# A decoder layer's cross attention with queries instead of keys held stationary, and its three programs joined into one

## The reference

```python
# 16 query heads, 4 key heads, HEAD_DIM 128; q and k normed and turned, k_full = context + own keys
scores = jnp.einsum('blhd,bmhd->bhlm', q, k_full) * scale + mask      # mask: 0 for context, causal for own keys
probs = jax.nn.softmax(scores, axis=-1)
out = jnp.einsum('bhlm,bmhd->blhd', probs, v_full)
```

## Time and profile before

| | us |
|---|---|
| median of 3 runs | 2986.56 |
| the profiled execution, its own time | 2984.8 |
| its span | 2982.8 |
| TensorE (PE) busy | 2906.3 (97%) |
| VectorE (DVE) busy | 1384.0 (46%) |
| ScalarE (ACT) busy | 1034.6 (35%) |
| GpSimd (POOL) busy | 186.6 (6%) |

### The profile page before, as it was taken

The page is one execution under the profiler, slowest core; times in us unless marked ns, Lnnn a source line. Parts: engine busy times, 40 slices in busy tenths (PEclk is TensorE's granted clock), DMA queues, the critical chain, the costliest instruction groups (busy, mean ns, idle before and its releaser), DMA issues. The chain is left out here.

```text
span 2982.8 us, 40563 instructions
## 1 busy us (share of the span) xinstructions
PE 2906.3 (97%) x15836; PEld 2775.5 (93%) x15836; DVE 1384.0 (46%) x1683; ACT 1034.6 (35%) x1499; POOL 186.6 (6%) x213
## 2 busy tenths in 40 slices
PE   8999999999999999999899999999999999999998
PEld 7899888899999999899799999999899999999997
DVE  3322233344454444578788888834522222222235
ACT  4322233332222223234476766722311121221222
POOL 0000000000000000200022322201000000000001
PEclk9999999999999999999899999999999999999999
DMA  4232223211111111022111112112111211111122
GB/s 170 87 108 81 79 79 129 74 49 56 43 47 52 56 44 69 29 88 69 53 62 57 56 61 63 40 53 102 57 56 56 71 56 57 60 67 56 56 72 99
DMA packets 88106, 203.03 MB, mean 68 GB/s; under 512 B 9376, under 2 KB 64260, under 8 KB 73832
## 3 DMA queue, kind: packets, MB, share of 16 engines
q1 hardware_dynamic: 88040, 202.12, 20.3%
HBM read 171.89 MB, written 30.21 MB: 68 GB/s over the span
## 5 line engine op out<-in xcount | busy, mean ns | idle before, releaser
L116 PE MATMUL PS<-XH,WH 128*128 128x400 f32 x2176 | 755.4, 347 | 10.6 <-DVE t_ROOM L1846 6.6
L118 PE MATMUL PS<-XH,WL 128*128 128x400 f32 x2176 | 746.5, 343 | 0.0
L117 PE MATMUL PS<-XL,WH 128*128 128x400 f32 x2048 | 703.5, 343 | 0.0
L116 PEld LDWEIGHTS PS<-XH,WH 128*128 128x128 f32 x2176 | 410.5, 189 | 15.8 <-issue 8.6
L118 PEld LDWEIGHTS PS<-XH,WL 128*128 128x128 f32 x2176 | 409.1, 188 | 0.1
L117 PEld LDWEIGHTS PS<-XL,WH 128*128 128x128 f32 x2048 | 384.5, 188 | 0.0
L1608 DVE TENSOR_TENSOR WL<-RAW,WH 128x1024 fp32r<-128x1024 f32 x86 | 105.4, 1225 | 524.2 <-ACT WH L1602 524.2
L86 ACT ACTIVATE WH<-RAW 128x1024 fp32r<-128x1024 f32 x120 | 126.9, 1058 | 552.0 <-PE PS L118 367.8
L92 DVE TENSOR_TENSOR WL<-RAW,WH 128x1024 fp32r<-128x1024 f32 x120 | 146.8, 1224 | 321.2 <-ACT WH L86 320.0
L1602 ACT ACTIVATE WH<-RAW 128x1024 fp32r<-128x1024 f32 x86 | 91.1, 1059 | 535.3 <-PE PS L118 530.4
L1560 DVE TENSOR_TENSOR XL<-a_E,XH 128x400 fp32r<-128x400 f32 (+1 forms) x224 | 174.0, 796 | 22.0 <-ACT XH L1504 22.0
(11 more groups left out here) (250 smaller groups left out, 5367.8 us busy)
## 6 DMA issues: line engine op xcount, KB each, us to landing
RAW<-weights_dram SPq DMA_DIRECT2D x111, 1024.0 KB, 4.8
a_KRAW<-keys_scratch SPq DMA_DIRECT2D x32, 411.0 KB, 3.3
a_VRAW<-values_scratch SPq DMA_DIRECT2D x32, 384.0 KB
R<-context_dram SPq DMA_DIRECT2D x8, 1352.0 KB, 6.5
R<-context_dram SPq DMA_DIRECT2D x7, 1536.0 KB, 7.1
values_scratch<-VS SPq DMA_DIRECT2D x40, 256.0 KB
keys_scratch<-KS SPq DMA_DIRECT2D x8, 768.0 KB, 6.1
keys_scratch<-KS SPq DMA_DIRECT2D x8, 676.0 KB, 5.3
```

Of the source, the lines that this page charges most:

```text
L116: pe.matmul(out, wh, xh[:, k, cols], start=(k == 0), stop=False)
L117: pe.matmul(out, wh, xl[:, k, cols], start=False, stop=False)
L118: mm = pe.matmul(out, wl, xh[:, k, cols], start=False, stop=(k == KT - 1))
```

## The change

The attention is written anew, and all stages stand in one block: each engine's attention instructions follow directly on its heads instructions, and the tail's on these. Per stage and head the queries are stationary for the full three-pass scores too, against all 824 key columns (822 and two masked ones) in two banks; the scores come out queries x keys. VectorE takes the negated maximum of a head; ScalarE's exponential takes it as its bias and gives the sum of the row from the same instruction. TensorE then transposes the exponentials, 4 heads x 7 chunks, by plain f32 transposes into PSUM; ScalarE copies the high part out, VectorE subtracts the low part; values are weighed with three matmuls per chunk. VectorE takes the reciprocal of the sums (100 x 4), GpSimd writes it on diagonals, one f32 matmul with ones spreads it to all partitions, ScalarE copies that out and VectorE multiplies. The values' low part moves from GpSimd to VectorE. Keys are loaded and split two stages ahead, values one. Scores of the next stage are made between the chunks of this one.

What TensorE issues:

```diff
+            def scores(b, v, j):
+                if j == 0:
+                    pe.wait_ge(k_lo, 4 * b + (v + 1))
+                    pe.wait_ge(q_lo, 4 * b + (v + 1))
+                pe.wait_ge(exped, 16 * b + (4 * v + j + 1))
...
+                for x, (q, key) in enumerate(((qh, kh), (qh, kl), (ql, kh))):
+                    for g in range(2):
+                        pe.matmul(out[:, g, :], q, key[:, g, :], start=(x == 0),
+                                  stop=(x == 2 and g == 0), skip_group_check=True)
+                pe.matmul(out[:, 1, HK - (KEYS_E - CTX):HK], SAME, MASK, start=False, stop=True,
+                          skip_group_check=True).then_inc(s_raw, 1)
+            def turn(b, v, k):
+                if k == 0:
+                    pe.wait_ge(exped, 16 * b + (4 * v + 4 + 2))
+                for j in range(GRP):
+                    mm = pe.transpose(c.PS[0:rows[k], turn_bank(v, k), j * T:(j + 1) * T],
+                                      E[:, slot(v, j), k * P:k * P + rows[k]], c.ID[0:T, 0:T])
+                mm.then_inc(t_raw, 1)
+            def weigh(b, v, k):
+                pe.wait_ge(e_lo, 28 * b + (KC * v + k + 1 + 2))
+                if k == 0:
+                    pe.wait_ge(v_lo, 4 * b + (v + 1))
+                    pe.wait_ge(o_out, 4 * b + (v + 1))
```

The instructions of VectorE and ScalarE that are new in kind:

```diff
+                dve.tensor_reduce(LOW[:, v % 2, j:j + 1], score_banks(j), AX.XY, ALU.max,
+                                  negate=True).then_inc(maxed, 1)
+                act.activation(E[:, slot(v, j), :].rearrange("p (g n) -> p g n", g=2),
+                               score_banks(j), ACT.Exp, bias=LOW[:, v % 2, j:j + 1], scale=1.0,
+                               accum_out=TOTAL[:, v % 2, j:j + 1]).then_inc(exped, 1)
+                act.activation(EHL[0][0:r, ring(v, k), :], c.PS[0:r, turn_bank(v, k), 0:GT],
+                               ACT.Copy).then_inc(e_hi, 1)
+                dve.tensor_tensor(EHL[1][0:r, ring(v, k), :], c.PS[0:r, turn_bank(v, k), 0:GT],
+                                  EHL[0][0:r, ring(v, k), :].bitcast(F32),
+                                  ALU.subtract).then_inc(e_lo, 1)
```

Two transpose banks, four rings of `EHL` and two pairs of score banks are in use. In the tail the last stage's output is multiplied behind the first two low parts of its input, and ScalarE's load of its tables is gone:

```diff
-                act.preload_act_table_set("natural_log_exp_and_others")
+            act.wait_ge(attention.o_out, attention.o_all - 1)
             for k in range(KT):
+                if k == 2:
+                    act.wait_ge(attention.weighed, attention.weighed_all)
                 act.activation(c.XH[:, k, :], qx[:, KV_N + k, :], ACT.Copy).then_inc(x_hi, 1)
...
                 attention_lo(k, None)
+                if k == 1:
+                    attention.last_output(dve)
```

More of the change, by code:

```diff
@@ L43 @@
 UNIT = KT * P
-KEY_A = 412
+KEYS_E = -(-KEYS // 4) * 4
 X_EARLY = 4
@@ new lines, in prepare, with gpsimd, diagonal, body @@
+        def prepare(pool):
+            pool.sem_inc(exped, 2)
+            pool.sem_inc(e_lo, 2)
+            pool.sem_inc(weighed, RING)
+            pool.sem_inc(o_out, 1)
+            pool.sem_inc(spread, 1)
+        def gpsimd(pool, heads_done):
+            pool.wait_ge(heads_done, 2 + 1)
+            pool.memset(KRAW[:, KEYS:KEYS_E], 0.0).then_inc(zeroed, 1)
+            pool.wait_ge(heads_done, 2 + QH_N + KV_N)
+            pool.memset(VRAW[:, KC - 1, :], 0.0).then_inc(zeroed, 1)
+            def diagonal(b, v):
+                pool.wait_ge(inverted, 4 * b + (v + 1))
+                if not (isinstance(b, int) and b == 0 and v == 0):
+                    pool.wait_ge(spread_raw, 4 * b + v)
+                pool.tensor_tensor(heads(DG[:]), c.ID[0:T, 0:T].unsqueeze(1)
+                                   .broadcast_to([T, GRP, T]),
+                                   INV[:, v % 2, :].unsqueeze(2).broadcast_to([T, GRP, T]),
+                                   ALU.mult).then_inc(diag, 1)
+            def body(b, first, last):
+                for v in range(KV_N):
+                    diagonal(b, v)
+            every_batch(pool, body)
@@ new lines, in tensor, with spread_inverse, body, ahead @@
+        def tensor(pe):
+            def scores(b, v, j):
[3 more added lines that the diff above has]
+                pe.wait_ge(exped, 16 * b + (4 * v + j + 1))
+                kh, kl = (x[:, v % 2, :].rearrange("p (g n) -> p g n", g=2) for x in KHL)
+                qh, ql = (x[:, v % 2, j * T:(j + 1) * T] for x in QHL)
+                out = score_banks(j)
+                for x, (q, key) in enumerate(((qh, kh), (qh, kl), (ql, kh))):
[7 more added lines that the diff above has]
+                    pe.wait_ge(exped, 16 * b + (4 * v + 4 + 2))
+                for j in range(GRP):
+                    mm = pe.transpose(c.PS[0:rows[k], turn_bank(v, k), j * T:(j + 1) * T],
[6 more added lines that the diff above has]
+                    pe.wait_ge(o_out, 4 * b + (v + 1))
+                r = rows[k]
+                vh, vl = (x[0:r, v % 2, k * HD:(k + 1) * HD] for x in VHL)
+                eh, el = (x[0:r, ring(v, k), :] for x in EHL)
+                out = c.PS[:, 6, 0:GT]
+                pe.matmul(out, vh, eh, start=(k == 0), stop=False)
+                pe.matmul(out, vh, el, start=False, stop=False)
+                pe.matmul(out, vl, eh, start=False, stop=(k == KC - 1)).then_inc(weighed, 1)
+            def spread_inverse(b, v):
+                pe.wait_ge(diag, 4 * b + (v + 1))
+                pe.wait_ge(spread, 4 * b + (v + 1))
+                pe.matmul(c.PS[:, 7, 0:GT], c.ONES[0:T, :], DG[:], start=True,
+                          stop=True).then_inc(spread_raw, 1)
+            def body(b, first, last):
+                for v in range(KV_N):
+                    nxt = after(b, v, 1, last)
+                    def ahead(j):
+                        if nxt is not None:
+                            scores(*nxt, j)
+                    ahead(0)
+                    turn(b, v, 0)
+                    turn(b, v, 1)
+                    ahead(1)
+                    weigh(b, v, 0)
+                    turn(b, v, 2)
+                    weigh(b, v, 1)
+                    turn(b, v, 3)
+                    weigh(b, v, 2)
+                    ahead(2)
+                    turn(b, v, 4)
+                    spread_inverse(b, v)
+                    weigh(b, v, 3)
+                    turn(b, v, 5)
+                    weigh(b, v, 4)
+                    ahead(3)
+                    turn(b, v, 6)
+                    weigh(b, v, 5)
+                    weigh(b, v, 6)
+            pe.wait_ge(tables, 2)
+            for j in range(GRP):
+                scores(0, 0, j)
+            every_batch(pe, body)
@@ L1597, in split_ahead_hi @@
+        done = Core()
+        done.weighed, done.weighed_all = weighed, KC * STAGES + RING
+        done.o_out, done.o_all = o_out, STAGES + 1
+        done.last_output = lambda dve: output(dve, B - 1, KV_N - 1)
+        return prepare, gpsimd, sync, scalar, vector, tensor, done
 def split_ahead_hi(c, act, j, t, m, off):
@@ L1609, in split_ahead_lo, with phase_tail @@
                       ALU.subtract).then_inc(c.w_lo, 1)
-def phase_tail(c, nc):
+def phase_tail(c, nc, sem_of, attention):
     PER = 24
@@ L1925, in decoder_layer @@
+        return prepare, gpsimd, sync, scalar, vector, tensor
 def decoder_layer(nc, c):
@@ new lines, in decoder_layer, with _ @@
+        tail = phase_tail(c, nc, own, attention[-1])
+        with nc.Block() as block:
+            @block.gpsimd
+            def _(pool):
+                context[0](pool)
+                heads[0](pool)
+                attention[0](pool)
+                tail[0](pool)
+                retention[0](pool)
+                attention[1](pool, heads[-1])
+                tail[1](pool)
+            @block.sync
+            def _(sp):
+                context[1](sp)
+                retention[1](sp)
+                heads[1](sp)
+                attention[2](sp, heads[-1])
+                tail[2](sp)
+            @block.scalar
+            def _(act):
+                context[2](act)
+                retention[2](act)
+                heads[2](act)
+                attention[3](act)
+                tail[3](act)
+            @block.vector
+            def _(dve):
+                context[3](dve)
+                retention[3](dve)
+                heads[3](dve)
+                attention[4](dve)
+                tail[4](dve)
+            @block.tensor
+            def _(pe):
+                context[4](pe)
+                retention[4](pe)
+                heads[4](pe)
+                attention[5](pe)
+                tail[5](pe)
```

969 lines of the change are left out of this document (440 added, 529 removed).

## The result

The changed kernel takes 3021.5 us (median of four, 3019.5 to 3025.3), the kernel before 2986.6 (2986.0 to 2988.3): ratio 1.0117, interval 1.010 to 1.0135. It is slower, by 35 us where 11 were forecast, and just outside the range. The profiled executions stand at 3019.5 (span 3017.8) and 2984.8 us, 34.7 apart.

A forecast was written before the change was run, and what follows sets the result against it. TensorE was taken to bound attention at 14.34 us a stage; 12.14 of work, lateness, 54 partitions and the sum made 14.92, with the seams +11.8 us on 2984.8: 2996.6, as median 2998, range 2970 to 3020.

The forecast's parts named there:

- clock 1.00: Sign of being right: TensorE's granted clock stays at full rate, 1.00, through the attention stretch.
- the walk: One attention stage followed through the fixed queue orders with hand-overs: 14.82 us, 14.92 with the exponential's sum.
- What bounded the kernel before: Attention before the change: TensorE's own work is the bound, 14.34 us a stage, 459 us for 32 stages.
- TensorE's work after, 12.14: Scores 4.97, transposes 3.01, weighing 3.82, spreading the inverse 0.34 us a stage; some 2 us less than before.
- Late places: Three weighings in a stage where TensorE waits for other engines: 0.54, 0.20 and 1.76 us in all.
- weigh 6: Weighing of a stage's last chunk, held up by VectorE's values' low part and maximum 3: late 1.69, in all 1.76 us.
- weigh 2: Weighing of chunk 2 in a stage, its turnaround longer than TensorE's work between: late 0.47, in all 0.54 us.
- weigh 4: Weighing of chunk 4 in a stage: late 0.13, in all 0.20 us.
- Sum's cost 0.1: The row sum taken by ScalarE's exponential: 0.1 us a stage assumed, ends 14.82 and 15.03 a stage.
- Seams: Attention's two ends: first turn at 1494.4, tail starting at 1966.6 against 1954.8 before in full-clock time; 9 us given back.
- clock rival: Transposes don't hold TensorE's full clock, which falls to 1.2 GHz: over 220 us more, 3220; chance 0.02.
- rival of a shorter turnaround: Values' low part and maximum 3 don't delay the last weighing so much: 14.2 us a stage, 2976; chance 0.22.

The follow-up runs named there:

- the last run: The changed kernel with the same instructions in another order in the TensorE, ScalarE and VectorE queues: 2927.7 us, ratio 0.9807 to the kernel before.
- the run with the filled wait: The changed kernel plus nine unread 400-column matmuls on TensorE before the last chunk's weighing in each stage that prepares a next one: 2995.3 us, ratio 1.0029.

## Why the prediction was wrong

The step that failed is "clock 1.00" beside a wait of 1.7 us a stage; it stands below under the clock. The other terms come first, in the order of the walk.

- **What bounded the kernel before**: TensorE alone, 14.34 us a stage. Right: what TensorE was given back was worth its full time as soon as nothing was late (the last run).
- **TensorE's work after, 12.14**: right in sum (the reordered kernel's stage of 12.3), by two errors that cancel, which is luck. The four transposes of a turn follow at some 0.085 us, not 0.111: from the first transpose at 1702.17 to the second matmul of the weighing behind it at 1702.72 are 0.55 us, and 0.37 without the one normal interval of 0.18 in it, where I had 0.44. The last, of 54 columns, costs 0.37 too, where I had 0.35: in all 0.4 a stage less. The plain f32 matmul that spreads the inverse appears as two matmuls and takes 0.70 (1706.07 to 1706.95, less one normal matmul), not 0.34: 0.36 more. Its 0.34 was the interval of the earlier trace rows, whose 16 records I took for 16 matmuls. They are 8: that code (`take_variance`, L490) issues one for each of 8 squares, and each gives two records, as the spread does (x2 in L1444's row). The row was misread, not the size.
- **Late places**: the cause of weigh 6's delay and the chain to it were right to 0.1 us, from scores 2 (1704.54) to weigh 6 (7.68 us later, walked 7.59). Its delay itself was walked at 1.69 and is 1.90: its predecessor starts at 1710.14, so weigh 6 could have started at 1710.32 and starts at 1712.22. The 1.73 of the profile counts only from the predecessor's modelled end. Counted in the same way weigh 2 is late by 0.50 (idle 0.29; walked 0.47), and weigh 4 not at all (walked 0.13). What was too long is the way from weigh 6 to the next scores 2: 6.88 us measured where the walk has 7.23, and four turns at 0.37 in place of 0.44 are 0.3 of it. So a stage is 14.56 for 14.92, 11 us in my favour over 31 stages.
- **Sum's cost 0.1**: confirmed, 0.10.
- **Seams**: turn 0 of stage 0 came at 1496.9, not 1494.4, as the heads phase ended 2.8 us later (1479.15 against 1476.35). Most of this too is the clock. The front's TensorE instructions are the same, and some 2 us of the 2.8 arise at two places where it was at half clock for longer: near 1233, and after a wait in the retention, where the rows before and after are

```profile
1153.09 1.95 PE L126 MATMUL PS<-ID,SQ 128*100 128x128 f32 x16 [1.93 <-ACT SQ L654]
1153.94 2.85 PE L126 MATMUL PS<-ID,SQ 128*100 128x128 f32 x16 [1.93 <-ACT SQ L654]
```

The half-clock stretch behind this wait stands in all nine traces of the changed kernel and its variants and in none of the three of the kernel before; why isn't known. The gap of 6.56 us before the tail is gone, as forecast (0.46 is left). The tail's start, 1961.2 in the run with the filled wait, was walked at 1966.6. The end of the tail took 3 us more in the changed kernel: its 8 variance matmuls (16 records) took 8.70 us instead of 5.64, at a clock of 0.66 in the 10 us around them, 5.64 again in the reordered kernel, 7.33 with the filled wait. Same instructions, same wait before them; only when they come differs.
- **The clock**: this is the step that failed. I wrote that TensorE would idle 1.7 us once a stage, and "clock 1.00" beside it, without asking what the one does to the other. The only clock rival was tied to the transposes, with 0.02, and was dismissed by 16 transposes at 1.00. That the transposes were not the danger is right: with the wait short or filled, stages with 28 to 48 transposes and a stream of 560 stayed at 1.00. But the row gave me the comfort that the clock was dealt with, and it could not give it. It held 1.93 us of idle TensorE at 1.00, and the same place is at half clock in eight of the twelve traces: it was one event that happened to go well. By the alternating stages even here every second wait does no harm. The clock cost 15 x 1.56 = 23 us in the stages and some 2 more in the last one, where I had nothing.
- **The sum of it**: by the profiled executions the forecast span was 2994.6 and the measured one 3017.8, 23.2 more. Turn 0 came 2.5 late; the 31 stages took 475.9 for 462.5 (23.4 of clock, less 10.0 by the shorter stage); the last stage took 3.0 more, 2.3 of it for the clock; from the tail's start on it was 1032.2, where the walk left 1028.0 and the kernel before had 1030.3. That the run with the filled wait lands within 3 us of 2998 is therefore in part luck: there 10.0 too much for the stages stands against 4.0 too little in front, 0.7 in the last stage and 3.8 in the tail.

The Trainium skill ("TensorE: Matmul & The Clock Gate", A second HAM failure mode: psum-queue depth-cycling) warns that short idle stretches between groups of matmuls can make the clock go up and down. This case's trace agrees (fifteen stages of 30), and it is the rule that I should have weighed in place of the one on transposes. The rule on transposes (the Trainium skill, "TensorE: Matmul & The Clock Gate", Part 4: PE-mode transpose) isn't borne out here: 560 transposes in a row ran at 1.00. They came when the clock was up already; whether transposes can raise it was not tried.

The rival of a shorter turnaround (0.22) named the place, the values' low part ahead of low 6, correctly. By itself the edit is worth 1.05 us a stage, in which I had put 0.7.

## What to carry to other kernels

When a forecast leaves TensorE with a wait of over a microsecond in each turn of a loop, price the clock with it: here the loss, 0.75 us a stage on average, was as large as the walk's terms for weigh 2 and weigh 4 together (0.54 and 0.20), appeared in no idle row, and could be had back by work without use in the gap. Taking work from the bounding engine pays only as far as the in-order queues of the others let it: the same instructions gave 3021 and 2928 us, and one low-urgency operation (values wanted a stage later) ahead of an urgent one cost 60. Read the granted clock by stage before attributing a slower stretch to work, and don't take one wait at full clock as a sign that waits of that length are safe.

## What the runs showed of the hardware

- The half-clock stretches of the stages lasted 3.4 us each (6.8 in the last stage) and began after the wait had ended, in the middle of dense work: 1.3 to 1.7 us after it in the changed kernel, 1.4 to 1.9 with two matmuls in the gap, 0.15 to 1.3 in the kernel before with a wait added. They came in exactly every second stage at waits of 1.36 and 1.73 us, in 12 of 29 stages at 1.88, and in none at 0.97 to 1.01. Why every second, and not each, isn't settled by these runs; nor is what besides the wait's length counts. Something does: the same instructions after the same wait of 1.93 us kept the clock in some executions and lost it in others.
- Back-to-back ordinary matmuls of 100 columns let the clock fall after 8.8 us and kept it at 1.2 GHz for the remaining 102; transposes of the same width did not, and fourteen such matmuls in a stage of others did no harm either.
- A transpose of 100 columns costs 0.086 us in a stream, an ordinary matmul of 100 columns 0.112 at full clock and 0.213 at half.
- The sum out of an exponential is a second instruction of 0.2 us on ScalarE; the four of a stage lengthened it by 0.1 us together.
